# A conditioned feed-forward block on one core: nine more weight tiles of the first chunk are transposed by the DMA queue

## What is computed

```python
x: (4, 1024, 512)   up_w: (4096, 512)   down_w: (512, 2048)   cond: (4, 128)
scale = cond @ norm_w.T + 1.0
h = x * (scale[:, None, :] * rsqrt(mean(x * x) + EPS))
u = h @ up_w.T
val, gate = split(u, 2, axis=-1)
h = val * gelu(gate)
hq = act_quant(h)                 # 8 bits, one scale for each row
wq = weight_quant(down_w)         # -1, 0, 1
y = hq @ wq.T + x
# second layer: a small bottleneck whose weights depend on cond
out = y + (relu(y @ Wd_b.T + bd) @ Wu_b.T + bu)
```

## Time and profile before

| | |
|---|---|
| median of 3 runs | 942.75 us |
| lowest, highest | 941.86, 942.82 us |
| the profiled execution | 943.0 us |
| its span, first to last instruction | 941.2 us |
| TensorE's share of the span | 99% |
| ScalarE's, VectorE's | 46%, 72% |
| granted TensorE clock | 1.00 |

### The profile page before, as it was taken

How to read it: one execution, slowest core, us unless ns; L and a number is a source line. 1 busy time by engine, 2 the same in 40 slices (tenths; PEclk the granted TensorE clock), 3 DMA queues, 4 the chain that set the end, 5 groups by cost and what they waited for, 6 DMA issues and landing times.

```text
span 941.2 us, 13789 instructions
## 1 busy us (share of the span) xinstructions
PE 933.6 (99%) x5266; PEld 464.4 (49%) x5266; DVE 675.3 (72%) x1030; ACT 437.6 (46%) x800; POOL 53.4 (6%) x53
## 2 busy tenths in 40 slices
PE   8999999999999999999999999999999999999998
PEld 6555544444444444444444444444444444455586
DVE  5778888766877696767877687757877685256766
ACT  6898677224731276214742166213742255214443
POOL 1000000000000000000000000000000000000564
PEclk9999999999999999999999999999999999999999
DMA  8899654564346543664347543664347534421584
GB/s 286 239 219 217 169 151 131 150 193 137 101 140 170 161 134 112 159 168 155 112 131 177 152 138 99 173 174 146 110 127 186 149 90 135 112 68 35 185 307 179
DMA packets 118810, 145.36 MB, mean 154 GB/s; under 512 B 51796, under 2 KB 57432, under 8 KB 118232
## 3 DMA queue, kind: packets, MB, share of 16 engines
q1 hardware_dynamic: 118744, 144.48, 53.2%
HBM read 112.72 MB, written 20.97 MB: 142 GB/s over the span
## 4 chain that ended last, share of the span: by engine, by line
PE 97%; ACT 1%; DMA 1%; DVE 0%; issue 0%; SPq 0%; DVEq 0%; ACTq 0%
PE bank L1088 23%; PE bank L1090 23%; PE bank L1089 23%; PE bank L1190 10%; PE bank L1147 6%; PE bank L1200 1%; PE bank L1327 1%; PE bank L1336 1%; PE bank L1068 1%; PE bank L1349 1%; PE bank L1357 1%; PE bank L1359 1%; PE bank L1358 1%; PE bank L1366 1%; DMA xn<-in_x 1%; PE bank L1367 1%
## 5 line engine op out<-in xcount | busy, mean ns | idle before, releaser
L1088 PE MATMUL bank<-x_split,w_hi 128*128 128x512 f16 x1016 | 385.4, 379 | 0.0
L1089 PE MATMUL bank<-x_split,w_hi 128*128 128x512 f16 x1016 | 385.2, 379 | 0.0
L1090 PE MATMUL bank<-x_split,w_lo 128*128 128x512 f16 x1016 | 385.2, 379 | 0.0
L829 DVE STREAM_TRANSPOSE delta_reg<-delta_reg 128x512 f32<-128x512 f32 x256 | 262.4, 1108 | 51.7 <-DMA delta_reg<-in_L_cond_Wdu 19.3
L643 ACT ACTIVATE g<-h 128x512 f32<-128x512 f32 x128 | 80.6, 630 | 301.6 <-DVE h L925 301.6
L1090 PEld LDWEIGHTS bank<-x_split,w_lo 128*128 128x128 f16 x1016 | 99.4, 98 | 120.0
L1088 PEld LDWEIGHTS bank<-x_split,w_hi 128*128 128x128 f16 x1016 | 99.4, 98 | 119.2 <-issue 6.6
L1089 PEld LDWEIGHTS bank<-x_split,w_hi 128*128 128x128 f16 x1016 | 99.4, 98 | 113.2
L925 DVE SCALAR_TENSOR_TENSOR h<-bank,desc,g 128x512 f32<-128x512 f32 x128 | 93.1, 727 | 81.7 <-issue 57.9
L627 ACT ACTIVATE g<-bank,desc 128x512 f32<-128x512 f32 x128 | 87.5, 683 | 118.1 <-PE bank L1090 117.9
L1190 PE MATMUL bank<-wqT,qreg 128*128 128x512 fp8e4 x448 | 101.3, 379 | 0.0
(11 more groups left out here) (175 smaller groups left out, 628.6 us busy)
## 6 DMA issues: line engine op xcount, KB each, us to landing
delta_reg<-in_L_cond_Wdd SPq DMA_DIRECT2D x128, 256.0 KB, 2.9
delta_reg<-in_L_cond_Wdu SPq DMA_DIRECT2D x128, 256.0 KB, 2.9
qreg<-in_L_cond_up_w SPq DMA_DIRECT2D x32, 256.0 KB, 4.7
xr<-in_x SPq DMA_DIRECT2D x30, 256.0 KB, 3.8
x_scratch<-xr SPq DMA_DIRECT2D x30, 256.0 KB, 3.2
xn<-in_x SPq DMA_DIRECT2D x7, 1024.0 KB, 5.7
h<-in_L_cond_down_w SPq DMA_DIRECT2D x4, 1024.0 KB, 7.3
delta_reg<-in_L_cond_down_w SPq DMA_DIRECT2D x8, 512.0 KB, 4.6
```

The lines of the kernel that those rows point to most:

```text
L829: dve.transpose(natT[:, t, k, :, :].rearrange("p a (r e) -> p e a r", e=4), nat[:, v % HALVES, :]).then_inc(nat_turned, 1)
L1088: pe.matmul(bank[:, :], w_hi[:, k, cols], xh[:, par, k, :], start=(k == 0), stop=False)
L1089: pe.matmul(bank[:, :], w_hi[:, k, cols], xl[:, par, k, :], start=False, stop=False)
L1090: mm = pe.matmul(bank[:, :], w_lo[:, k, cols], xh[:, par, k, :], start=False, stop=(k == KD - 1))
```

## The change

Nine pairs' gate halves (3 to 8 and 13 to 15, `GATES`) take the way of the value halves. ScalarE makes the high half as the rows lie, into a second buffer of two slots (`g_parts`, two unused slots of `delta_reg`); VectorE makes the low half; SP issues two more transposing transfers for each (`turn_gate`), placed right behind `turn_value` of the same pair. TensorE's four transposes of these tiles are gone, as are ScalarE's copy from the bank and VectorE's scaling and subtraction. TensorE's gate product of such a tile waits for both transfers (`gate_turned`). The gate halves of the pairs 9 to 12 stay as they were. ScalarE's instruction waits until the transfers of the tile two before in the buffer have landed, and SP's `load_up` waits for VectorE's low half.

```diff
--- before.py
+++ after.py
@@ -159,8 +159,15 @@
         SPLIT = 3
         w_parts = delta_reg[:, 2 * NATT - 2:2 * NATT, :].rearrange("p s e -> p (s e)").bitcast(F16).rearrange("p (n v d) -> p n v d", n=2, v=2)
 
+
+        GATES = (3, 4, 5, 6, 7, 8, 13, 14, 15)
+        g_parts = delta_reg[:, 4:6, :].bitcast(F16).rearrange("p n (v d) -> p n v d", v=2)
+
         def halves_done(jj, p):
-            return 2 * jj + p + 1 if jj < SPLIT else SPLIT + jj + 1
+            return 2 * jj + p + 1 if jj < SPLIT else 2 * SPLIT + len([m for m in range(SPLIT, jj + 1) if m not in GATES])
+
+        def turned_halves(jj, halves):
+            return halves if jj < SPLIT else () if jj in GATES else (0,)
 
         def w_bank(jj):
             return (VAL[1], GATE[1]) if jj == 1 else (Y, TB)
@@ -194,6 +201,8 @@
         w_squared, w_expd, w_scaled, w1_scaled, w_turned = sem("w_squared"), sem("w_expd"), sem("w_scaled"), sem("w1_scaled"), sem("w_turned")
         w_hi_done, w_lo_done = sem("w_hi_done"), sem("w_lo_done")
         value_high, value_low = sem("value_high"), sem("value_low")
+        gate_high, gate_low = sem("gate_high"), sem("gate_low")
+        gate_turned = [sem(f"gate_turned{i}") for i in range(2)]
         value_turned = [sem(f"value_turned{i}") for i in range(2)]
         rows_in = [sem(f"rows_in{i}") for i in range(4)]
         rows_summed = sem("rows_summed")
@@ -321,6 +330,8 @@
                     sp.wait_ge(w_turned, halves_done(jj - 3, 1))
                 if jj >= 3 + SPLIT:
                     sp.wait_ge(value_low, jj - 2 - SPLIT)
+                if jj - 3 in GATES:
+                    sp.wait_ge(gate_low, GATES.index(jj - 3) + 1)
                 for i in range(2):
                     r = (jj + FT * i) * P
                     sp.dma_start(upn(jj, i), up_w[r:r + P, :]).then_inc(upn_in[jj % 3], 16)
@@ -331,6 +342,14 @@
                 sp.dma_start(w_hi[:, :, cols], w_parts[:, jj % 2, 0, :], transpose=True).then_inc(value_turned[jj % 2], 16)
                 sp.wait_ge(value_low, jj - SPLIT + 1)
                 sp.dma_start(w_lo[:, :, cols], w_parts[:, jj % 2, 1, :], transpose=True).then_inc(value_turned[jj % 2], 16)
+
+            def turn_gate(jj):
+                m = GATES.index(jj)
+                cols = slice((FT + jj) * P, (FT + jj + 1) * P)
+                sp.wait_ge(gate_high, m + 1)
+                sp.dma_start(w_hi[:, :, cols], g_parts[:, m % 2, 0, :], transpose=True).then_inc(gate_turned[m % 2], 16)
+                sp.wait_ge(gate_low, m + 1)
+                sp.dma_start(w_lo[:, :, cols], g_parts[:, m % 2, 1, :], transpose=True).then_inc(gate_turned[m % 2], 16)
 
             def load_rows(dt):
                 if dt == 3:
@@ -421,6 +440,8 @@
                         load_rows(3)
                     if first and SPLIT <= j + 2 < FT:
                         turn_value(j + 2)
+                    if first and j + 2 in GATES:
+                        turn_gate(j + 2)
                     for i in loads_in(c, j):
                         load_pieces(i)
                     if first and j == 11:
@@ -578,8 +599,12 @@
                         act.wait_ge(value_turned[jj % 2], 32 * ((jj - SPLIT) // 2))
                     act.wait_ge(w_expd, 3 * jj + 3)
                     act.activation(w_parts[:, jj % 2, 0, :], upn(jj, 0), ACT.Copy, scale=winv[:, 2 * jj:2 * jj + 1]).then_inc(value_high, 1)
-                    halves = (0,)
-                for p in halves:
+                if jj in GATES:
+                    m = GATES.index(jj)
+                    if m >= 2:
+                        act.wait_ge(gate_turned[m % 2], 32 * (m // 2))
+                    act.activation(g_parts[:, m % 2, 0, :], upn(jj, 1), ACT.Copy, scale=winv[:, 2 * jj + 1:2 * jj + 2]).then_inc(gate_high, 1)
+                for p in turned_halves(jj, halves):
                     i = 1 - p
                     ft = jj + FT * i
                     act.wait_ge(w_turned, halves_done(jj, p))
@@ -750,7 +775,7 @@
                 dve.wait_ge(w_expd, 3 * jj + 3)
 
             def w_scale(jj, halves=range(2)):
-                for i in (1 - p for p in (halves if jj < SPLIT else (0,))):
+                for i in (1 - p for p in turned_halves(jj, halves)):
                     m = 2 * jj + i
                     dve.tensor_scalar(upn(jj, i), upn(jj, i), winv[:, m:m + 1], None, ALU.mult).then_inc(w_scaled, 1)
 
@@ -762,8 +787,12 @@
                     dve.wait_ge(value_high, jj - SPLIT + 1)
                     dve.scalar_tensor_tensor(w_parts[:, jj % 2, 1, :], upn(jj, 0), winv[:, 2 * jj:2 * jj + 1], w_parts[:, jj % 2, 0, :],
                                              ALU.mult, ALU.subtract).then_inc(value_low, 1)
-                    halves = (0,)
-                for p in halves:
+                if jj in GATES:
+                    m = GATES.index(jj)
+                    dve.wait_ge(gate_high, m + 1)
+                    dve.scalar_tensor_tensor(g_parts[:, m % 2, 1, :], upn(jj, 1), winv[:, 2 * jj + 1:2 * jj + 2], g_parts[:, m % 2, 0, :],
+                                             ALU.mult, ALU.subtract).then_inc(gate_low, 1)
+                for p in turned_halves(jj, halves):
                     i = 1 - p
                     ft = jj + FT * i
                     cols = slice(ft * P, (ft + 1) * P)
@@ -1052,7 +1081,7 @@
         @block.tensor
         def _(pe):
             def turn_w(jj, halves=range(2)):
-                for p in halves if jj < SPLIT else (0,):
+                for p in turned_halves(jj, halves):
                     i = 1 - p
                     if jj == 1:
                         pe.wait_ge(w1_scaled, p + 1)
@@ -1214,7 +1243,10 @@
                     if first and j == 0:
                         first_products()
                         continue
-                    if first:
+                    if first and j in GATES:
+                        m = GATES.index(j)
+                        pe.wait_ge(gate_turned[m % 2], 32 * (m // 2 + 1))
+                    elif first:
                         pe.wait_ge(w_lo_done, halves_done(j, 0))
                     if not (first and j < 2):
                         pe.wait_ge(gelu_done, n - 1)
```

## The result

The changed kernel takes 955.45 us in the median of 4 runs (955.09 to 957.79); the kernel before takes 942.31 us in the runs beside it. The ratio is 1.0144, with a 95% interval of 1.0131 to 1.0158: 13.1 us slower. The profiled execution took 957.79 us, so it lies 2.3 us above the median.

What follows compares the result with a forecast made beforehand. TensorE bounds the kernel, busy 99% of the span, with SP's issuing nearly full behind it. SP's 23.2 us added less 12.9 of waiting, plus 3.1 to land, delay gate tile 15 by 7.9 us: 942.75 + 7.9 = 950.7 us, range 948.0 to 957.0.

Steps and rivals of the forecast that it cites:

- The mechanism: First chunk: SP, nearly full already, issues nine more pairs of transposing transfers, so gate products wait; 7.9 us slower.
- SP's sum: SP's queue, first chunk: 23.2 us of issues added less 12.9 us of waiting given up, counted from 100.33 us.
- the forecast 110.6: Time in us at which SP begins gate tile 15's low half: 100.33 + 23.2 - 12.9.
- What is added: SP's queue: nine pairs of transposing transfers at 2.58 us a pair, 23.2 us.
- What SP gives up: SP's waiting for three releasers in the first chunk, 12.9 us, all given up to the added issues.
- The last step, from the transfer to the product: Gate tile 15: low half lands 3.1 us after issue start, at 113.7; TensorE's product, before at 105.84, begins 7.9 us later.
- A late `load_up`: SP's `load_up`, moved behind the added issues: due in ScalarE's next step but one, a few us harmless.
- The DMA engines' rival: The 16 DMA engines become the bound, stretching issues and landings: 17.0 us slower, 959.8 us; chance 0.10.
- 0.5 us of all sixteen engines: Estimated DMA engine cost of one transposing transfer, from a share of 0.30 over 2.6 us; eighteen cost 9 us.
- Where the waits stand: TensorE waits ahead of gate products at tiles 5 to 8 and 13 to 15, none at 9 to 12; 11 to 13 us.
- The kept gain: Rival: added issues fit beside SP's other work, TensorE keeps its 4.45 us saving, 938.3 us; chance 0.06.
- The clock's rival: Rival: TensorE's longer waits lower its clock to 1.2 GHz; 5.2 us more behind the last stall, 955.9 us; chance 0.06.

Runs made afterwards that it cites:

- the kernel with the filler: Changed kernel plus 32, 64 and 80 small matmuls ahead of TensorE's wait at gate tiles 3, 6 and 13: 957.27 us, ratio 1.0161.
- with three tiles: Changed kernel with only gate tiles 13, 14 and 15 on the transfers' way, 3 to 8 as before: 946.21 us, ratio 1.0035.

## Why the prediction was right, and where its size was off

It said slower by 7.9 us, because SP would be full; it is 13.1 us slower, inside the range of 948 to 957 and 4.8 us above the forecast.

**The mechanism stands.** The loss is the count of issues on SP: kept with a quarter of the bytes (953.6 us), gone with half the issues and all the bytes (943.0 us). SP's timeline is full from 28 to 111 us, as forecast, and an issue put at 1.26 us measured 1.27 (0.04 us between two). TensorE's waits were forecast at 11 to 13 us and measured 12.4, but that agreement is luck: the forecast was 7.9 us of lateness and 4.45 saved, while the trace has 14.4 us of lateness, 4.45 saved and 6.2 of slower matmuls between them.

**The terms that were too small are in SP's sum.** From the start of its first value pair to the start of its last transfer SP takes 72.8 us before (27.50 to 100.33) and 89.8 after (26.78 to 116.55). These are 16.9 us more, where the sum has 23.2 - 12.9 = 10.3. The pair starts 0.7 us earlier, so the last transfer is 6.0 us behind the forecast 110.6. The missing 6.6 us are in both terms:

- *What is added*, put at 23.2 us, measured 26.9. The eighteen issues themselves take 23.6. The rest is mostly issues that are held, that is, whose row is longer than usual: three take 3.9 us more than usual, two in the kernel before 1.5. The three weight loads of step 11 take 2.1 us instead of 1.4.
- *What SP gives up*, put at all of 12.9 us, measured 10.0 (12.2 us without an issue before, 2.2 after). 1.6 us of the 2.2 lie ahead of the last value pair, and they come through TensorE: ScalarE's half of value tile 15 stands behind the gelu of gate tile 13, whose product began 11.9 us late and ran at the lower clock.

```profile
111.36 0.69 ACT L652 ACTIVATE g<-bank,desc 128x512 f32<-128x512 f32 x1 [4.88 <-PE bank L1119]
111.95 0.71 ACT L601 ACTIVATE delta_reg<-qreg,winv 128x512 f16<-128x512 f32 x1
```

The second term is no general limit: without TensorE's wait SP gives up all but 0.4 us. The larger error is in the first, where every issue was costed as an undisturbed one.

**The last step, from the transfer to the product,** was also different. The sum has gate tile 15 landing at 113.7 and TensorE waiting for it. It lands at 119.05 (116.55 + 2.5), and TensorE begins it at 120.24 without a wait, 1.2 us later, because it came late itself. Its last long wait was at tile 13, whose product it began at 94.15 before:

```profile
94.15 0.38 PE L1088 MATMUL bank<-x_split,w_hi 128*128 128x512 f16 x1
```

The low half of tile 13 landed 4.7 us after the start of its issue, where the sum took 3.1:

```profile
L352 SPq DMA_TRANSPOSE w_lo<-delta_reg x1: 1272/1272/1272, 101.3 to 101.3; - x1
...
DMA to landing us min/median/max: 4.7/4.7/4.7
```

So the product began at 106.02, 11.9 us late. Then 3.0 us of slower matmuls, less the 0.43 saved between the two tiles, make the 14.4 us at tile 15.

**A late `load_up`** was called harmless. In the changed kernel ScalarE waits 4.6 us for the loads of `up_w`, where the trace of before has 1.5, and no wait of TensorE follows from it:

```profile
ACT xr L594 <- DMA qreg<-in_L_cond_up_w: 4.6, 4, 2.9
```

Where TensorE doesn't wait for the gate transfers it does matter: ScalarE waits 9.1 us and TensorE 3.5 for tiles scaled late. The forecast of 945 us for that kernel had looked at value tile 15 alone and had nothing for this, nor for the wait of 3.7 us behind the 1 MB load.

**The DMA engines' rival** holds in places. The 1 MB load of `down_w` rows at 47.59 us is followed by two transfers; the issue of the second takes 3.50 us, 2.2 more than usual. As the bound of the whole it is out, by the run with a quarter of the bytes. The prediction's 0.5 us of all sixteen engines for a transfer does not follow from its row either: 0.30 of 2.6 us for two gives 0.4.

**Where the waits stand.** The prediction had them at the tiles 5 to 8 and 13 to 15 and none at a value tile; they are at 3, 6, 8 and 13, and 0.8 us at value tile 11.

**The kept gain** was a rival at 938.3 us. Even without any transfer it is 940.4, since VectorE's scaling and the value tiles stand right behind TensorE's 4.45 us.

**The clock's rival** came true in the rows and not in the time: 0.53 of full speed behind a wait of 4.7 us, and no gain where the wait was filled. The prediction's place for it, behind the last wait, was right: there are 3.0 us of slower matmuls behind tile 13's. But in the kernel with the filler SP was no earlier, so waits of 0.5 and 1.1 us came up at the tiles 14 and 15 in their place. The Trainium skill, page TensorE: Matmul & The Clock Gate, section What's actually happening, has an idle array fall to half its clock. The changed kernel's trace agrees for waits of 2.1, 3.8 and 4.7 us and shows no fall after one of 1.0. The length of the wait does not decide it alone: with three tiles the granted clock reads 1.00 behind a wait of 3.0 us (94 to 100 us), and with a quarter of the bytes behind one of 3.7 (54 to 66 us).

**The page on issue time.** By the Trainium skill, page DMA: Bandwidth & Descriptors, section Issuing engines are not separate DMA queues, the time to initiate a DMA is usually small beside the DMA. For transposing transfers the runs speak against it: 1.23 us of issue for a transfer of 128 columns that lands after 2.3.

## What to carry to other kernels

A queue that only issues transfers has a load that no share of busy time shows. Before something is moved to it, add up its issues over the stretch and set them against the time in which it issues nothing, one step of the loop at a time. Below that time the additions here cost little, above it nearly their full length. Take that time from the queue's timeline: a list of waits can name a later tile's increment. Leave room for issues that are held behind a large load, and cost every load that is queued behind the new issues by who reads it next. Where the issue's cost is fixed, lay the destinations side by side and issue once.

## What the hardware showed that was not expected

- The issue of a transposing transfer from SP takes 1.23 us for 128 columns, 1.20 to 1.27 for 512 and 1.23 for 1024 (float16, 128 rows).
- An issue can take far longer: 3.50 us for the second transfer behind a 1 MB load (3.20 without TensorE's wait, 3.26 with a quarter of the added bytes), up to 3.72 right behind a transposing transfer of 1024 columns.
- With the plain loads in GpSimd's queue the transposing transfers land after 6.5 us in the median (up to 11.0), with all in SP's queue after 2.5.
